# A Mamba-2 block and a mixture of experts: order of one group's work, of the head and of the last tiles changed

## What is computed

```python
xn = (x - mean) / sqrt(var + 1e-5)
# branch 1, Mamba-2: 16 heads of 64, state 128
z, xBC, dt = split(xn @ in_proj_w.T)          # 1024, 1280, 16 columns
dt = softplus(dt + dt_bias)
x_, B, C = split(silu(conv4(xBC)))            # causal, 4 taps, per channel
state = state * exp(sum dt*A) + sum_s exp(decay_s) * dt_s * x_s * B_s   # per chunk
y = C @ state_before * exp(decay) + (mask(C @ B) * exp(segment decays)) @ (dt*x_) + D * x_
y = y * silu(z); y = y * rsqrt(mean(y*y) + 1e-5) * norm_w
branch1 = y @ out_proj_w.T
# branch 2: 8 experts, 2 of them for each token, F = 192
branch2 = sum over 2 experts of p_e * (silu(xn @ gate_e) * (xn @ up_e)) @ down_e
```

## Time and profile before

| what | us |
|---|---|
| median of the runs | 737.36 |
| the profiled execution | 735.81 |
| its span | 734.0 |
| PE busy (matmul) | 647.0, 88% |
| VectorE busy | 531.2, 72% |
| ScalarE busy | 374.4, 51% |
| GpSimd busy | 311.2, 42% |
| mean granted PE clock | 0.967 |
| a group of two scan tiles, 276.60 to 336.10 | 59.5 |
| first transpose of tile 0, of tile 15 | 47.47, 502.96 |
| first hidden product on VectorE (L1322) | 555.05 |

### The profile page before, as it was taken

The page is one execution under the profiler, slowest core; times in us unless marked ns, Lnnn a source line. Parts: engine busy times, 40 slices in busy tenths (PEclk is TensorE's granted clock), DMA queues, the critical chain, the costliest instruction groups (busy, mean ns, idle before and its releaser), DMA issues.

```text
span 734.0 us, 12653 instructions
## 1 busy us (share of the span) xinstructions
PE 647.0 (88%) x4189; PEld 530.3 (72%) x4190; DVE 531.2 (72%) x1116; ACT 374.4 (51%) x787; POOL 311.2 (42%) x223
## 2 busy tenths in 40 slices
PE   4857899999999999999999989884868999999992
PEld 3747778768777786777877868563547889989981
DVE  4966879977987997996998798877947744444430
ACT  3673963763754566366376373636035644444441
POOL 1110335353444452543535325245434666565642
PEclk9979999999999999999999999998878999999996
DMA  8830304032230430421403303095086577677663
GB/s 258 327 134 31 115 1 145 30 115 89 86 116 30 144 117 5 153 99 34 144 31 116 115 2 115 1 229 145 5 287 189 96 135 134 124 122 129 121 100 43
DMA packets 32050, 80.91 MB, mean 110 GB/s; under 512 B 4800, under 2 KB 10048, under 8 KB 29824
## 3 DMA queue, kind: packets, MB, share of 16 engines
q1 hardware_dynamic: 22176, 55.22, 22.6%
q0 software_dynamic: 9056, 21.50, 16.2%
q10 hardware_dynamic: 768, 3.54, 2.0%
HBM read 60.45 MB, written 19.79 MB: 109 GB/s over the span
## 4 chain that ended last, share of the span: by engine, by line
PE 41%; DVE 34%; issue 9%; ACT 5%; POOL 4%; DMA 4%; SPq 0%; DVEq 0%; POOLq 0%; ACTq 0%
PE pg L1610 11%; DVE xs L916 7%; PE pi L1419 7%; PE pd L1623 7%; PE po L1458 6%; DVE y L1196 3%; DVE step_acc L884 3%; PE py L1496 2%; DMA e<-cs_d 2%; PE px L1593 2%; PE py L1503 2%; DVE carry L1294 2%; DVE xs L931 2%; POOL ln L461 2%; ACT m L647 1%
## 5 line engine op out<-in xcount | busy, mean ns | idle before, releaser
L1419 PE MATMUL pi<-xh,whl 128*128 128x256 f32 x1152 | 167.2, 288 | 8.1 <-DVE zs L922 7.2
L1419 PEld LDWEIGHTS pi<-xh,whl 128*128 128x128 f32 x1152 | 148.3, 191 | 12.4 <-issue 11.1
L1458 PE MATMUL po<-wo,y 128*128 128x512 f32 x256 | 116.0, 607 | 8.1 <-DVE cbm L1219 8.1
L916 DVE SCALAR_TENSOR_TENSOR xs<-raw,conv_w,xs 128x256 f32<-128x256 f32 x240 | 112.5, 534 | 11.6 <-ACT xs L622 11.6
L1458 PEld LDWEIGHTS po<-wo,y 128*128 128x128 f32 x256 | 48.5, 194 | 64.0 <-issue 55.3
L1419 PE MATMUL pi<-xl,whl 128*128 128x256 f32 x576 | 92.2, 282 | 0.0
L531 POOL DMA_INDIRECT out<-yo,idx x39 | 62.0, 1590 | 56.5 <-ACT yo L776 31.8
L647 ACT ACTIVATE m<-m,cs_tok 128x128 f32<-128x128 f32 x256 | 79.7, 389 | 0.5
L1419 PEld LDWEIGHTS pi<-xl,whl 128*128 128x128 f32 x576 | 79.0, 190 | 0.0
L506 POOL TENSOR_TENSOR carry<-carry,cd 128x1024 f32<-128x1024 f32 x15 | 29.0, 1932 | 90.4 <-PE py L1496 90.4
L1610 PE MATMUL pg<-ew,xgh 128*128 x312 | 66.6, 357 | 0.7 <-issue 0.7
(11 more groups left out here) (203 smaller groups left out, 1200.1 us busy)
## 6 DMA issues: line engine op xcount, KB each, us to landing
m<-cs_d SPq DMA_DIRECT2D x16, 1024.0 KB, 5.6
e<-cs_d SPq DMA_DIRECT2D x32, 256.0 KB, 4.8
w_as_read<-in_w_in SPq DMA_DIRECT2D x9, 512.0 KB, 7.6
res<-in_x SPq DMA_DIRECT2D x16, 256.0 KB, 2.7
out<-o SPq DMA_DIRECT2D x16, 256.0 KB, 2.0
ew<-in_w_gu SPq DMA_DIRECT2D x5, 768.0 KB, 8.3
xin<-in_x SPq DMA_DIRECT2D x6, 512.0 KB, 3.4
xn_d<-xin SPq DMA_DIRECT2D x6, 512.0 KB, 2.8
```

The source lines that it names most:

```text
L916: dve.scalar_tensor_tensor(out=xs[par][:, b, :], in0=raw[:, b, k:k + GT], scalar=conv_w[:, b, k:k + 1], in1=xs[par][:, b, :], op0=ALU.mult ...
L1419: mm = pe.matmul(bank[:, hf, :], whl[:, weight(g, n), lo, k, hf * P:(hf + 1) * P], xx[:, k, :], start=k3 == 0, stop=k3 == 11)
L1458: mm = pe.matmul(po[:, :], y[:, b, :], wo[:, b, :], start=b == 0, stop=b == XB - 1)
```

## The change

Three things are reordered; no instruction's work is changed.
1. TAKEN becomes five pairs in the even tile and four in the odd one, so conv3 is made (PE, ScalarE, VectorE) at the end of the even tile. The softplus steps of the odd tile, which stood 2, 3, 3, 3 and 7 together, the last 13 behind the carry add, become 10 before `decayed(1)`, 4 before `own(1)` and 4 at the tile's end.
2. Head: the gate of pair 4, the router's rows and the scores come before the decay kernel of tile 0 on ScalarE; its last two quarters come behind pair 5. PE makes pairs 5 to 8 together, behind the product of C and B.
3. Last tiles: in tiles 14 and 15 squares and variance of the tile before come behind `diag(0)` and `own(0)`; all of `table_given` comes in tile 15 behind cbm; the split of expert 0 leaves tile 15 for the place behind it, and experts 0 to 3 are split on VectorE before the last `variance` and `finish`; the last square comes before the casts `high` and the split of expert 3; the first `gate_up` comes before the last `squares`.

```diff
@@ -61,7 +61,7 @@
 PAIRS = ((True, 0), (True, 1), (True, 2), (False, 0), (True, 3), (True, 4), (False, 1), (False, 2), (False, 3))
 NP = len(PAIRS)
 NX, NZ = CB // 2, XB // 2
-TAKEN = ((0, 1, 2, 3), (4, 5, 6, 7, 8))
+TAKEN = ((0, 1, 2, 3, 4), (5, 6, 7, 8))
 
 FIRST = (0, 1, 2, 4, 5, 3, 6, 7, 8)
 RING = 8
@@ -684,19 +684,16 @@
             weight_high(5)
             stage(0, 3)
             group_high(1)
+            stage(0, 4)
+            weight_high(6)
+            router_rows(1)
+            gated(0, NX - 1)
+            scores(1)
             decay_factors(0)
             kernel_part(0, 0, 4)
-            stage(0, 4)
-            kernel_part(0, 1, 4)
-            router_rows(1)
-            gated(0, NX - 1)
-            kernel_part(0, 2, 4)
-            scores(1)
-            weight_high(6)
             step_exp(1)
             weight_high(7)
-            kernel_part(0, 3, 4)
-            weight_high(8)
+            kernel_part(0, 1, 4)
 
             def fold(first, last):
 
@@ -719,7 +716,11 @@
                     for e in range(3):
                         load_expert(act, e)
                 if t == 0:
-                    for n in range(NX, NP):
+                    weight_high(8)
+                    stage(0, 5)
+                    kernel_part(0, 2, 4)
+                    kernel_part(0, 3, 4)
+                    for n in range(NX + 1, NP):
                         stage(0, n)
                 for n in taken[:1]:
                     stage(g + 1, n)
@@ -789,10 +790,10 @@
 
             gate_up_high(act, 2)
             down_high(act, 2)
+            square(T - 1)
             high(0, 0)
             high(1, 1)
             gate_up_high(act, 3)
-            square(T - 1)
             gate_up_high(act, 4)
             down_high(act, 3)
             for j in range(7):
@@ -1163,10 +1164,10 @@
             stage(0, 2)
             stage(0, 3)
             group_low(1)
-            decay_differences(0)
             stage(0, 4)
             weight_low(5)
             gated(0, NX - 1)
+            decay_differences(0)
             time_steps(1, 0, 2)
             weight_low(6)
             time_steps(1, 2, 5)
@@ -1229,7 +1230,8 @@
                         statistics(g + 2)
                         spread(g + 2)
                 if t == T - 1:
-                    table_given(5)
+                    for n in (0, 3, 4, 5):
+                        table_given(n)
                     table_place(1)
                 dve.wait_ge(me, t + 1)
                 dve.wait_ge(cbm_done, t + 1)
@@ -1263,27 +1265,27 @@
                 if t == T - 1:
                     decayed(0)
                     experts_of_tiles()
-                    gate_up_low(dve, 0)
-                    down_low(dve, 0)
                     table()
                 if c == 0 and g + 1 < G:
                     decay_rows(g + 1)
                 if more:
                     decayed(0)
                 if c == 1 and prepares:
-                    time_steps(g + 2, 0, 2)
+                    time_steps(g + 2, 0, 10)
                 if c == 0 and prepares:
                     group_low(g + 2)
                 decayed(1)
-                if t:
+                if 0 < t < T - 2:
                     variance(t - 1)
                 own(0)
+                if t >= T - 2:
+                    variance(t - 1)
                 for n in taken[2:3]:
                     stage(g + 1, n)
                 if t:
                     finish(t - 1)
                 if c == 1 and prepares:
-                    time_steps(g + 2, 2, 5)
+                    time_steps(g + 2, 10, 14)
                 own(1)
                 if t == T - 1:
                     break
@@ -1293,19 +1295,12 @@
                     sl = carry[:, 4 * half:4 * half + 4, :, :].rearrange("p b a d -> p (b a d)")
                     dve.tensor_tensor(sl, pxb[half][:, :, :].rearrange("p b l -> p (b l)"), sl,
                                       ALU.add).then_inc(cadd, 1)
-                if c == 1 and prepares:
-                    time_steps(g + 2, 5, 8)
-                if t == T - 2:
-                    for n in (0, 3, 4):
-                        table_given(n)
                 for n in taken[3:4]:
                     stage(g + 1, n)
-                if c == 1 and prepares:
-                    time_steps(g + 2, 8, 11)
                 for n in taken[4:]:
                     stage(g + 1, n)
                 if c == 1 and prepares:
-                    time_steps(g + 2, 11, 18)
+                    time_steps(g + 2, 14, 18)
 
             for done in (hg_done, x_lo):
                 dve.sem_inc(done, CR)
@@ -1331,15 +1326,16 @@
                 dve.tensor_tensor(hl[par][:, :, :], ph[par], hh[par][:, :, :].bitcast(F32),
                                   ALU.subtract).then_inc(h_lo, 1)
 
-            gate_up_low(dve, 1)
+            gate_up_low(dve, 0)
             low(0, 0)
             low(1, 1)
-            down_low(dve, 1)
+            down_low(dve, 0)
+            for e in (1, 2):
+                gate_up_low(dve, e)
+                down_low(dve, e)
+            gate_up_low(dve, 3)
             variance(T - 1)
             finish(T - 1)
-            gate_up_low(dve, 2)
-            down_low(dve, 2)
-            gate_up_low(dve, 3)
             gate_up_low(dve, 4)
             for j in range(9):
                 body(j, j % 2, j // 2)
@@ -1517,9 +1513,7 @@
                     for b in range(4):
                         tr = pe.transpose(pxb[half][:, b, :], xs[par][:, 4 * half + b, tok], ident[:, :])
                     tr.then_inc(xtr, 1)
-                if t == 0:
-                    stage(0, 5)
-                else:
+                if t:
                     stages(0)
                 pe.wait_ge(btok_done, t + 1)
                 if t and c == 0 and g + 1 < G:
@@ -1530,9 +1524,8 @@
                 if t == T - 3:
                     count_picks()
                 if t == 0:
-                    stage(0, 6)
-                    stage(0, 7)
-                    stage(0, 8)
+                    for n in range(NX, NP):
+                        stage(0, n)
                     stages(0)
                     pe.wait_ge(cbm_done, 1)
                     cumulate(1)
@@ -1556,12 +1549,14 @@
                     off(0)
                 stages(2)
                 off(1)
-                if t:
+                if 0 < t < T - 2:
                     if c == 0 and g + 1 < G:
                         pe.wait_ge(rows_copied, g + 2)
                     squares(t - 1)
                 pe.wait_ge(m_done, t + 1)
                 diag(0)
+                if t >= T - 2:
+                    squares(t - 1)
                 if t == T - 1:
                     diag(1)
                     break
@@ -1662,8 +1657,8 @@
             turn(0, 0, 0)
             turn(1, 1, 0)
             project(T - 1)
+            gate_up(0, 0, expert_of(0))
             squares(T - 1)
-            gate_up(0, 0, expert_of(0))
             for j in range(9):
                 body(j, j % 2, j // 2)
             by_twos(pe, body, 9)
```

## The result

The changed kernel takes 740.79 us (median of 20 runs, 737.14 to 744.35) against 737.24 us of the kernel before on the same chips (20 runs): ratio 1.0056, 95% interval 1.0039 to 1.0073. It is slower, by some 4 us. The forecast was 737.1, no change; the time lies at the upper end of its range. The profiled execution has a span of 739.4 us, 5.4 more than the 734.0 of before.

A forecast was written before the change was run, and what follows sets the result against it. Took VectorE's order, not its sum, to set the 59.5 us group, with PE's floor at 57.5. Terms 4.5 - 0.6 - 0.4 + 0.3 + 0.5 - 4.5 = -0.2 us gave 737.1 us; range 731 to 741.

The forecast's parts named there:

- tile 15's term: Tile 15 to the first hidden tile: project(15) ends near 543.7, hidden tile starts at 550 to 551; -4.5, ends -2.0 and -6.0.
- Groups and tiles 1, 12, 13: Five-four split with regrouped softplus: five groups +4.5 (ends -5.5, +6.5), tile 1 -0.6, tiles 12 and 13 -0.4.
- The router's wait: Odd tile: PE's router product waits 1.9 for xdt, behind conv3's taps on VectorE.
- the carry wait: Odd tile's start: PE's 1.00 wait for the carry add goes, since PE has 2.9 us more to do first.
- the even tile's idle time: Even tile of a group: the idle 1.0 us only changes its place, to the cumulative sum and second off product.
- blocked by L514: Even tile's start: GpSimd's gate multiply holds the last four softplus steps; -1.0 a group if they were not blocked.
- Rival B: Last softplus steps run free, even tile's idle time goes: another 1.0 in the five groups; 728 to 730, chance 0.12.
- Tile 14: Squares behind the diagonal product remove a 2.08 wait, but decays e come 2.8 later; +0.5, ends -2.0 and +4.0.
- Rival C: Tile 14: decays queue behind expert weights, e over 14 us after the tile's start, tile +4; 740.6, chance 0.24.
- Head: Tile 0 starts near 44.5, but the kernel multiply comes 0.3 later; +0.3, ends -2.5 and +1.5.
- the 2.91 in tile 12: Tile 12: PE's wait for the decay multiply; what the changed split moves is taken up there.

The follow-up runs named there:

- e1: Changed kernel with only the split put back to four pairs in the even tile and five in the odd: 726.45 us, 0.9881 to the kernel before.
- e6: Kernel before with only the split changed, five pairs in the even tile and four in the odd: 756.13 us, 1.0290.
- e5: Kernel before with only the softplus steps regrouped (ten, four, four), split, head and last tiles as before: 726.37 us, 0.9878.
- e4: Changed kernel with the head's order put back as before, all else changed: 739.09 us, 1.0052 to the kernel before.
- e7: Kernel before with only the last tiles' part of the change (squares, table products, variance, expert subtractions, last square): 734.70 us, 0.9999.
- e3: Changed kernel, but SyncE loads experts 3 to 5 only after the first two gathers have landed: 738.87 us, 1.0049 to the kernel before.
- e13: Kernel before with the last tiles' part alone, plus the first two gathers landed before experts 3 and 4 are loaded: 732.24 us, 0.9949.
- e8: Changed kernel with the split back to four and five and the two gathers landed before experts 3 and 4 load: 724.23 us, 0.9859.
- e10: Changed kernel with the weight loads of experts 0 to 2 issued behind e's exponential in tile 14: 741.15 us, 1.0069 to the kernel before.
- e2: Changed kernel, but VectorE makes the odd tile's xdt before conv3's taps, split as changed: 733.11 us, 0.9967 to the kernel before.
- e11: e8, and in even tiles the output step finish(t - 1) moved behind the carry add: 746.51 us, 1.0162 to the kernel before.
- e14: e11 with the next tile's decay kernel load put ahead of the output's store in SyncE's queue in even tiles: 723.94 us, 0.9835.
- e9: Changed kernel with GpSimd's gate multiply on a quarter of its columns, the other gating left out: 730.37 us, 0.9910 to the kernel before.
- e12: Changed kernel with one pair's 24 matmuls done twice in tile 12, where PE waits for the decay multiply: 741.35 us, 1.0086.

## Why the prediction was wrong

The step that failed is tile 15's term (below). Put into the sum as measured it alone turns -0.2 into +5.2; the two traces differ by 5.4, the medians by 3.6. The misses of the other stages nearly cancel: groups -2.1, head +1.3, tile 14 -0.3, expert tiles +1.4, for which the forecast had nothing.

Four kernels give the main parts of the change as a square. The changed kernel and e1 have the head's and the last tiles' part too, the other three don't:

| | split 4 and 5 | split 5 and 4 |
|---|---|---|
| softplus spread | 1.000 (before) | 1.029 (e6) |
| softplus regrouped | 0.988 (e5; e1) | 1.0056 (changed) |

**Groups and tiles 1, 12, 13 (+3.5 forecast, +1.4 in the traces): right mechanism, but one sum over two large parts.** The router's wait was forecast at 1.9 and is 1.84, the carry wait went, the even tile's idle time became 0.39 and 0.36; +0.9 a group forecast, +0.6 seen. The head's part is worth nothing in the ratios (e4), and the last tiles' part is worth nothing with four pairs (e7). As far as the parts add up, this part's share of the ratio is then the whole +4 us; no run has split and softplus alone. What the prediction did not see is what it consists of: -9 from the softplus and, on top of it, +13 from the split (in the other order, +21 from the split in e6 and -17 from the softplus). I held the regrouping to be blocked by L514 wherever it stood. With four pairs in the even tile it is not: one more gate pair lies between the carry add and the last steps, they begin behind L514's end (e5), and a group falls from 59.5 to 58.0. Rival B's mechanism was right, for a kernel without the split.

**Tile 15 to the first hidden tile (-4.5 forecast, +0.9 measured): the step that failed.** That project(15) would end near 543.7 took the second gathered block to arrive as before. The prediction itself had finish(14), and the loads of experts 3 and 4 behind it, come some 2 us earlier, with the gathers only 0.6; it did not price that the two would meet. Measured, the loads are 1.7 earlier and the gathers are issued as before; project(14) is 3.4 earlier, not 5. The block came 4.4 later against the tile's start, project(15) 4.4 later, and six of VectorE's subtractions stood behind it. With the loads held back the first hidden tile is at 49.2 (e3), 2.9 less than before, inside the -2 to -6 of the forecast; in the whole time -0.5% with four pairs (e13 against e7), nothing sure with five (e3). The collision is thus shown as the cause of this term's miss; that it is also what made the whole kernel slower is not shown. The expert tiles are 1.0 and 0.9 longer with the loads held back in e13 and e8, and 0.9 shorter in e3; why stays open.

**Tile 14 (+0.5 forecast, +0.2 measured): size right, cause right in part.** e was forecast 11.5 us after the tile's start and came at 11.6. The 2.8 us by which L511 is later are real (SyncE's queue has e's load 0.8 us after the tile's start, before it was 2.1 ahead of it). But the weights, to which the prediction put e's lateness, are only 1.9 of it: without them e came at 9.7 (e10). Why the load then takes 9 us in e10, when the page puts its median at 5.2, stays open; the decay kernel's 1 MB and the table's load are issued 2.7 and 3.3 us ahead of it there. Rival C gave 740.6, close to the result, through e landing over 14 us after the start and tile 14 at +4. Neither happened: that its time came out is luck.

**Head (+0.3 forecast): within the noise.** e4 and the changed kernel are alike. With the head of before and four pairs tile 1 starts at 88.7 or 88.8 in e5, e7 and e13, but at 86.6 in the trace that the prediction was made from; so the +1.6 in the comparison above can be chance. The +3.9 of PE's busy time are in the head and tile 0 (2.0), in tile 12 (1.2) and in the expert tiles (0.9).

**What no term held: the clock behind a wait.** The prediction counted the 2.91 in tile 12 as taken up. Behind tile 12's wait of 2.9 to 3.0 the matmuls run for some us at the lower clock in seven profiled executions (before, changed, e2, e4, e7, e10, e13), and at the full clock in an eighth (e3). Behind waits of 2.4 to 2.6 both are found: full in tile 13 of before (2.54) and of e1 (2.55), slow in four of e6's six. Behind 1.84 the clock mostly stays, but not at 219.71 in e10 and 411.75 in e6. The Trainium skill, page "TensorE: Matmul & The Clock Gate", section "HAM oscillation — how this bites in real kernels", says that a wait between bursts of matmuls can put the array back to its lower clock, so that the next burst starts at it. The traces agree that it can: sixteen matmuls took 1.97 in place of 1.09 behind the changed kernel's 2.97. They also show that it need not: 1.09 behind e3's 2.99. Where the clock falls, the wait costs more than its length: tile 12 took 35.4 with it and 32.6 without. e6 pays this in four of its five groups (PE busy 58.7 to 60.1; 57.5 in the other and before); the changed kernel's groups don't (tiles 2 to 11: 287.3 busy, 287.6 before). What decides it from one execution to the next stays open.

## What to carry to other kernels

Price the parts of a change one by one, even where they are edited together: a gain of 1.2% was hidden under a loss that the sum netted against it. When an engine's step comes earlier, list what it releases in the DMA queues and whom those transfers meet (e3, e13), and when it comes later, what stands behind it in the queue (e11, e14). Look behind each long wait of the matmul engine at the granted clock, and in more than one execution: behind about 3 us of waiting the matmuls of tile 12 lost another 2.8 us in one kernel and nothing in another with the same instructions there.

## What the runs showed of the hardware

- Tile 12 with the same instructions and a wait of 2.97 to 3.00 us took 35.3 to 35.6 us at a granted clock of 0.90 (changed kernel, e4, e10) and 32.6 at 1.00 (e3).
- A softplus step on VectorE took 1.97 us while GpSimd's L514 ran (changed kernel) and 0.19 just behind its end (e5).
- Moving 0.74 us of VectorE's work behind the carry add made the kernel 3% slower than e8 through the order of a DMA queue (1.0162 against 0.9859); with that order mended it is at 0.9835.
- Six DMA issues on ScalarE between two exponentials held the second one 2.25 us (e10).
- The same head with five pairs brings tile 1 at 91.1 to 93.9 in six profiled executions (the changed kernel, e2, e3, e9, e10, e12), with four at 88.1 to 90.8 (e1, e8, e11, e14). One profiled execution can't settle a term of that size there.
